# Layer norms between VectorE and ScalarE in a cross-attention and FFN kernel: passes moved, two waits placed elsewhere, a new end

## The chip, the cores and the metric

The kernel runs on one core of one Trainium2 chip. The metric is the device time of one execution in microseconds. Three runs of the kernel before give a median of 678.73 us (675.15 to 682.0).

## The reference

What is computed, for 8 batch rows of 100 query tokens and 722 context tokens, model width 512, 16 heads of 32:

```python
x = x + xattn(layernorm(x), ctx, ctx)      # q, k, v projections with bias, 16 heads
#   scores = q k^T / sqrt(32);  attn = sparsemax(scores);  out = (attn v) Wo + bo
h = layernorm(x)
x = x + sqrt((h @ cos(theta + theta_noise))**2 + (h @ sin(phi + phi_noise))**2)
# layernorm(x) = (x - mean) / sqrt(var + 1e-5), no gain, no bias
```

## The kernel before, in words

**Tiling.** A batch row is 100 tokens on 100 partitions. Its context is padded to 726 and cut into KC = 6 pieces of CK = 121. K, Q and V are made per batch; K and V with operands split in two float16 terms (three matmuls for each product, line 463), the output projection (`wo`, line 514) and the FFN (`wcos`, `wsin`, line 531) in float32. The 16 heads of a batch are handled in two parts of 8. A part `i` is batch `i // 2`, heads 0 to 7 (even `i`) or 8 to 15 (odd `i`); there are NH = 16 parts.

**Phases.** Every engine has its own instruction stream, written out by hand over the same list of phases `i` = -1 to 17, with semaphores between them. `b, odd = divmod(i, 2)`. In phase `i` TensorE multiplies the scores of part `i + 1`, VectorE finds the sparsemax thresholds of part `i`, and TensorE and ScalarE attend part `i - 1`. An odd phase also makes the first half of K and all of Q of batch `b + 1`, and the second layer norm's transposes and the FFN of batch `b - 1`. An even phase makes the second half of K and all of V of batch `b`, and the output projection of batch `b - 1`.

**TensorE** (`block.tensor`). `k_of`, `v_of`, `q_of`, `o_of` and `ffn_of` are generators that yield after each chunk of 128 contracted elements. `attend(i - 1)` yields 13 units: first `tau` (line 600: the thresholds are transposed into three more rows of the queries), then six blocks of scores, transposed (`st`, line 612, 8 matmuls), and six mixes with V (`mix`, line 583, 16 matmuls), each mix standing one block behind. Between the units stands `fill`: chunks of V in an even phase; in an odd one Q, the transposes of the normalised x1 (`x2T_of`, line 487) and the FFN. At the end of every phase `sum_flags(i)` (lines 542 and 544) sums VectorE's marks `over` over the partitions. Results go to two rings in PSUM, `ring1` (3 slots: projections) and `ring2` (2 slots: scores, blocks, tau), and ScalarE frees a slot by reading it (`one_read`, `two_read`).

**VectorE** (`block.vector`). For each head it takes the 8 largest of each of 16 pieces of the scores (`maxes`, line 952), then `thresholds(i)` does four turns over these candidates and marks, in line 988, which are above the threshold (`flag_ready`). In the next phase `read_flags` and `settle` look whether a head needs all its 722 scores after all. Three heads do in these inputs: they are refined one after the other (line 1029), two of them in phase 4 and one in phase 11, while TensorE waits in line 600 for `verified`. VectorE also does both layer norms: `stats` (bn_stats, bn_aggr, lines 928 and 930) and `normalise` (reciprocal and `(x - mean) * inv`, lines 934 and 936). For the first norm (`ln1`, tile xq, batch `b + 1`) they stand after head 4 and after the thresholds of the even phase; for the second (`ln2`, tile x1, batch `b - 1`) after heads 3 and 5 of the odd phase.

**ScalarE** (`block.scalar`) reads PSUM: K (lines 700, 704), V, Q and the scores S (`copy`, line 692), relu of the blocks to pT (line 817), attended values to aT (line 800). It makes the high float16 half of the context (`high_ctx`), the square root of the norms' variance (`ln_sd`, line 769), and square and root of the FFN (lines 782, 786).

**GpSimd** (`block.gpsimd`) makes the low halves (`low_ctx` line 340, `low_k` line 348, `low_q`), splits the thresholds (`split_tau`, lines 388 to 396), adds the bias to the residual (`residual`, line 362), makes x1 (`attended_x`, line 369), the FFN's sum of squares (line 374) and the output (`y_of`, line 379). SyncE's queue issues the transfers: kst, the context, xq, xr, and the store of `att`.

Two lines say how TensorE weaves an odd phase:

```python
fill = chain(itertools.islice(queries, 3), x2, queries, ffn)
for n, _ in enumerate(units):
    run(fill, (2, 1, 1, 1, 1, 0, 1, 0, 1, 0, 0, 0, 0)[n])
```

## Time and profile before

| | |
|---|---|
| median of 3 runs | 678.73 us (675.15 to 682.0) |
| profiled execution | 676.18 us |
| its span | 674.4 us |
| mean granted TensorE clock | 0.915 of full |
| chain that ended last, by engine | PE 49%, DVE 26%, issue 11%, ACT 7%, SPq 4%, DMA 2%, POOL 1% |
| longest kinds of TensorE's waits | line 600 42.3 us in 3; line 542 for VectorE 11.4 us in 6 |

The span runs from the first to the last instruction that the profiler shows; the time of the execution has 1.8 us more around it. The chain is followed back from the last instruction to what released it each time. PE is TensorE, PEld its weight loads, DVE VectorE, ACT ScalarE, POOL GpSimd, SPq the queue that SyncE feeds. A time in brackets in a list by time is how long the engine had stood idle, with what released it; "issue" is idle time for which the profile shows no releaser. A granted clock of 1.00 is 2.4 GHz, 0.50 is 1.2 GHz.

### The profile page before, as it was taken

To read this page: it belongs to the slowest core of one execution; us is meant where nothing else is said; L and a number is where in the kernel's file an instruction comes from. 1 tells how busy PE (TensorE), PEld (TensorE's weight loads), DVE (VectorE), ACT (ScalarE), POOL (GpSimd) and SP (SyncE) were. 2 spreads that over 40 slices of the span, in tenths; PEclk is the share of its full clock that TensorE was granted. 3 is DMA by queue.
4 is the path that set the end of the run, shared out by engine and by line. 5 is a ranking of instruction groups with operands and counts; after the bars stand their busy time and mean duration, and the time that the engine had idled before them with its cause. 6 is when DMAs were issued, how large, how long until landed. Compare 5 with 4: busy or idle time off the path is not lost.

```text
span 674.4 us, 14485 instructions
## 1 busy us (share of the span) xinstructions
PE 571.3 (85%) x4648; PEld 336.7 (50%) x4648; DVE 573.3 (85%) x2900; ACT 378.0 (56%) x657; POOL 189.0 (28%) x239
## 2 busy tenths in 40 slices
PE   2686999999913999899999999991899999988675
PEld 1343665656502655565556555651556565645431
DVE  5699999978967999999999999995999999999400
ACT  3674568767511667566756676661466666554321
POOL 2711322332220250435133422342024431310301
PEclk9968987999965999999999999996899999996768
DMA  9863022302230103130323022302203020300000
GB/s 309 273 173 91 16 63 74 96 7 62 84 84 0 31 11 98 55 98 5 85 69 105 0 61 89 103 11 61 76 9 98 20 54 27 80 7 9 13 1 12
DMA packets 33506, 44.25 MB, mean 66 GB/s; under 512 B 8386, under 2 KB 26818, under 8 KB 33415
## 3 DMA queue, kind: packets, MB, share of 16 engines
q1 hardware_dynamic: 32332, 41.16, 21.4%
q10 hardware_dynamic: 1088, 2.10, 0.9%
q8 instruction: 37, 0.61, 0.4%
q14 instruction: 49, 0.39, 0.2%
HBM read 23.77 MB, written 1.64 MB: 38 GB/s over the span
## 4 chain that ended last, share of the span: by engine, by line
PE 49%; DVE 26%; issue 11%; ACT 7%; SPq 4%; DMA 2%; POOL 1%; DVEq 0%; POOLq 0%; ACTq 0%
PE ring L463 29%; DVE cand L952 7%; PE mix_bank L583 3%; PE ring L612 3%; DVE dif L966 3%; PE ring L514 3%; PE ring L558 3%; DVE f_sum L975 3%; SPq L255 3%; DVE over L969 3%; ACT S L692 3%; PE ring L531 2%; DVE n_over L977 2%; DVE dif L970 2%; PE ring L501 1%
## 5 line engine op out<-in xcount | busy, mean ns | idle before, releaser
L952 DVE MAX8 cand<-S 100x8 f32<-100x45 f32 (+1 forms) x2048 | 223.5, 195 | 2.1 <-issue 0.4
L463 PE MATMUL ring<-wv,ctx 128*121 128x512 f16 x576 | 154.5, 390 | 0.0
L463 PE MATMUL ring<-ctx,wk 128*128 128x361 f16 x768 | 125.7, 323 | 4.7 <-DVE ctx L1118 4.7
L817 ACT ACTIVATE pT<-ring 121x800 f32<-121x800 f32 x96 | 80.5, 839 | 72.3 <-PE ring L612 71.6
L692 ACT ACTIVATE S<-ring 100x722 f32<-100x722 f32 x128 | 95.5, 773 | 32.6 <-PE ring L558 32.6
L463 PEld LDWEIGHTS ring<-ctx,wk 128*128 128x128 f16 x768 | 75.1, 99 | 50.0 <-issue 7.1
L340 POOL TENSOR_TENSOR ctx<-ctx_f,ctx 128x484 f16<-128x484 f32 x42 | 51.5, 1225 | 149.8 <-ACT ctx L692 149.4
L463 PEld LDWEIGHTS ring<-wv,ctx 128*121 128x121 f16 x576 | 71.4, 136 | 34.0 <-issue 7.7
L348 POOL TENSOR_TENSOR ks<-k_f,ks 128x361 f16<-128x361 f32 x64 | 57.9, 905 | 79.6 <-ACT k_f L704 76.7
L558 PE MATMUL ring<-kst,qst 96*100 96x361 f16 x256 | 65.1, 348 | 11.5 <-DMA kst<-ks 8.9
L612 PEld LDWEIGHTS ring<-qst,kst 99*121 99x121 f16 x768 | 59.3, 147 | 29.7 <-issue 13.8
L700 ACT ACTIVATE ks<-ring,bk_c 128x361 f16<-128x361 f32 x64 | 36.0, 563 | 65.3 <-PE ring L463 65.3
L612 PE MATMUL ring<-qst,kst 99*121 99x100 f16 x768 | 64.3, 231 | 2.9 <-ACT qst L692 2.9
L583 PE MATMUL mix_bank<-pT,v 121*32 121x100 f32 x1536 | 56.8, 269 | 1.9 <-ACT aT L800 1.2
L558 PEld LDWEIGHTS ring<-kst,qst 96*100 96x100 f16 x256 | 30.8, 133 | 55.3 <-issue 21.5
L692 ACT ACTIVATE qst<-ring 96x800 f16<-96x800 f32 (+1 forms) x32 | 25.7, 829 | 49.6 <-PE ring L600 45.9
L966 DVE TENSOR_TENSOR dif<-cand,tau 100x256 f32<-100x256 f32 (+1 forms) x64 | 51.3, 801 | 2.2
L583 PEld LDWEIGHTS mix_bank<-pT,v 121*32 121x32 f32 x1536 | 34.0, 115 | 35.4 <-issue 30.7
L975 DVE TENSOR_REDUCE f_sum<-dif 100x8 f32<-100x256 f32 (+1 forms) x64 | 49.7, 777 | 0.0
L600 PE MATMUL ring<-ident,tt 100*3 100x100 f16 x128 | 9.5, 225 | 46.0 <-issue 42.3
L374 POOL TENSOR_TENSOR sq<-sq 100x512 f32<-100x512 f32 x8 | 10.1, 1264 | 112.9 <-ACT sq L782 112.9
L969 DVE TENSOR_SCALAR over<-dif 100x256 bf16<-100x256 f32 (+1 forms) x64 | 38.4, 601 | 2.2
(124 smaller groups left out, 722.9 us busy)
## 6 DMA issues: line engine op xcount, KB each, us to landing
kst<-ks SPq DMA_DIRECT2D x384, 45.1 KB, 1.9
ctx_f<-in_ctx SPq DMA_DIRECT2D x45, 242.0 KB, 2.9
xq<-in_x SPq DMA_DIRECT2D x8, 200.0 KB
xr<-in_x SPq DMA_DIRECT2D x8, 200.0 KB
out_y<-att SPq DMA_DIRECT2D x8, 200.0 KB
S<-in_L_xattn_Wk ACTq DMA_DIRECT2D x1, 1024.0 KB, 6.9
wq<-in_L_xattn_Wq ACTq DMA_DIRECT2D x1, 1024.0 KB, 11.4
wcos<-in_L_ffn_theta SPq DMA_DIRECT2D x1, 1024.0 KB, 10.4
```

Of the source, the lines that this page charges most:

```text
L340: pool.tensor_tensor(ctx2[:, 1, :, at], ctx_f[:, n % 3, :, :], ctx2[:, 0, :, at], ALU.subtract).then_inc(ctx_lo_ready, 1)
L348: pool.tensor_tensor(ks[:, n % 2, 1, at], k_f[:, u % 2, :], ks[:, n % 2, 0, at], ALU.subtract).then_inc(k_lo_ready, 1)
L463: last = nc.tensor.matmul(psum, lhs(c, i), w(c, j), start=(c == 0 and n == 0), stop=(c == DC - 1 and n == 2))
L558: last = nc.tensor.matmul(psum[0:L, half, 0:HALF], qst[0:3 * DH, b % 2, HH * part + h, :], kst[0:3 * DH, i % 3, h, half * HALF:(half + 1) ...
L583: last = nc.tensor.matmul(mix_ps[DH * j:DH * (j + 1), :], v[0:CK, i % 3, kc, DH * (G * g + j):DH * (G * g + j + 1)], pT[0:CK, st_unit(i, g ...
L612: last = nc.tensor.matmul(psum[0:CK, c, j * L:(j + 1) * L], kst[0:99, i % 3, G * g + j, kc * CK:(kc + 1) * CK], qst[0:99, b % 2, HH * part ...
L692: return nc.scalar.activation(dst, src, ACT.Copy, **kw)
L817: nc.scalar.activation(pT[0:CK, u % 3, :, :], src, ACT.Relu).then_inc(two_read, 1)
L952: last = nc.vector.max(pieces[:, h, :, n], S[0:L, HH * (i % 2) + h, cuts[n]:cuts[n + 1]])
L966: n = counted(nc.vector.tensor_tensor(dif[:, :, 0:E], cand[:, :, 0:E], t3.broadcast_to([L, HH, E]), ALU.subtract))
L969: n_mask = counted(nc.vector.tensor_scalar(over[:, :, 0:E], dif[:, :, 0:E], 0.0, None, ALU.is_ge))
L975: counted(nc.vector.reduce_sum(f_sum[:, :], dif[:, :, 0:E], AX))
```

## The change

1. **Layer norms on ScalarE.** For ln1 of batches 1 to 7 and ln2 of batches 0 to 6 ScalarE does `centre` (a pass that sums x times -1/D into the mean with its results going to a tile nobody reads, one that subtracts the mean, one that sums the squares, and the root; each waits for the one before) and later `scale_x` or `scale_x1` (one pass, times the reciprocal). VectorE only makes the reciprocals (`invert`), after head 7 of the even phase (ln1) and after head 5 of the odd one (ln2). The first ln1 and the last ln2 stay on VectorE.
2. **Two waits.** TensorE sums the marks of an odd phase after the first four chunks of K of the next phase, no longer at the end of its own. GpSimd waits for the marks of the even phase before the last three of its six `low_ctx`.
3. **New end.** In the last attended phase the four chunks of `wo` stand between the units (each waits for its own aT), the FFN of batch 6 moves behind all units of its phase, and VectorE makes the last x1 straight from PSUM, and the last two additions, where ScalarE and GpSimd did.

The diff, cut to its core:

```diff
@@ gpsimd
-                    if 0 <= b - 1 < B:
+                    if 0 <= b - 1 < B - 1:
                         sum_squares(b - 1)
...
                         for kc in range(KC):
+                            if kc == KC // 2:
+                                pool.wait_ge(flag_ready, 2 * b + 1)
                             low_ctx(b + 1, kc)
                     if b > 0:
                         residual(b - 1)
+                    if 0 < b < B:
                         attended_x(b - 1)
-            y_of(B - 1)
@@ tensor
             def o_of(b):
...
-                pe.wait_ge(aT_ready, DC * (b + 1))
                 psum = slot1(("o", b))[0:L, :]
                 for c in range(DC):
+                    pe.wait_ge(aT_ready, DC * b + c + 1)
...
-                    fill = chain(itertools.islice(queries, 3), x2, queries, ffn)
+                    idle = iter([None] * (0 if b + 1 < B else 2))
+                    fill = chain(itertools.islice(queries, 3), x2, queries, idle, ffn)
...
                     weave(heads, fill, 1)
-                    if 0 <= i < NH:
-                        sum_flags(i)
                 else:
                     if b < B:
                         run(k_of(b, 2, 0), 4)
+                    if i > 0:
+                        sum_flags(i - 1)
+                    if b < B:
                         run(k_of(b, 2, 1), 4)
...
+                    attended_o = o_of(b - 1) if b > 0 else iter(())
                     run(fill, 4)
+                    if b == B:
+                        run(attended_o, 1)
                     for n, _ in enumerate(units):
                         run(fill, 2 if n == 0 else 1)
+                        if b == B and n in (0, 10):
+                            run(attended_o, 1)
                     weave(heads, fill, 1)
-                    if b > 0:
-                        run(o_of(b - 1), 4)
+                    run(attended_o, 4)
@@ scalar
+            def ln_link(ins):
+                ins.then_inc(ln_step, 1)
+                ln_steps[0] += 1
+                act.wait_ge(ln_step, ln_steps[0])
+
+            def centre(src, dst, mv, sd, done):
+                ln_link(nc.scalar.activation(unread[:, :], src, ACT.Copy, scale=-1.0 / D, accum_out=mv[:, 0:1]))
+                ln_link(nc.scalar.activation(dst, src, ACT.Identity, bias=mv[:, 0:1]))
+                ln_link(nc.scalar.activation(unread[:, :], dst, ACT.Square, accum_out=mv[:, 1:2]))
+                nc.scalar.activation(sd[:, 0:1], mv[:, 1:2], ACT.Sqrt, bias=eps_t[:, :], scale=1.0 / D).then_inc(done, 1)
+
+            def centre_x1(b):
+                act.wait_ge(x1_ready, b + 1)
+                centre(x1[:, :], x2n, mv2, sd2, ln2_sd)
+
+            def scale_x1(b):
+                act.wait_ge(ln2_inv, b + 1)
+                nc.scalar.activation(x2n, x2n, ACT.Identity, scale=sd2[:, 1:2]).then_inc(x2n_ready, 1)
...
-                    if 0 <= b - 1 < B:
-                        ln_sd(b - 1, mv2, sd2, ln2_stat, ln2_sd)
+                    if 0 <= b - 1 < B - 1:
+                        centre_x1(b - 1)
+                    if b == B:
+                        ln_sd(mv2, sd2, ln2_stat, ln2_sd)
                     run(units, 3)
+                    if 0 <= b - 1 < B - 1:
+                        scale_x1(b - 1)
                     if 0 <= b - 1 < B:
                         x2T_of(b - 1)
...
                     if b + 1 < B:
-                        ln_sd(b + 1, mv1, sd1, ln1_stat, ln1_sd)
+                        centre_x(b + 1)
                     run(units, 2)
...
-                    if b > 0:
+                    if b + 1 < B:
+                        scale_x(b + 1)
+                    if 0 < b < B:
                         o_of(b - 1)
@@ vector
+            def invert(b, sd, sd_done, done):
+                dve.wait_ge(sd_done, b + 1)
+                nc.vector.reciprocal(sd[:, 1:2], sd[:, 0:1]).then_inc(done, 1)
...
+            def last_x():
+                dve.wait_ge(one_full, one["o", B - 1] + 1)
...
+                nc.vector.tensor_tensor(x1[:, :], ring1[0:L, one["o", B - 1] % 3, :], xr[:, :], ALU.add).then_inc(one_read, 1)
...
                     if h == 3 and i > 0:
                         read_flags(i - 1)
-                    if h == 3 and odd and b >= 1:
-                        ln2_stats(b - 1)
                     if h == 4 and i > 0:
                         settle(i - 1)
                     if h == 5 and odd and b >= 1:
-                        ln2_apply(b - 1)
-                    if h == 4 and not odd and b + 1 < B:
-                        ln1_stats(b + 1)
+                        invert(b - 1, sd2, ln2_sd, ln2_inv)
+                    if h == HH - 1 and not odd and b + 1 < B:
+                        invert(b + 1, sd1, ln1_sd, ln1_inv)
                 thresholds(i, found)
                 if i == 0:
                     part_turns(1, wsin)
-                if not odd and b + 1 < B:
-                    ln1_apply(b + 1)
             read_flags(NH - 1)
             settle(NH - 1)
-            ln2_stats(B - 1)
-            ln2_apply(B - 1)
+            last_x()
+            last_norm()
+            last_y()
```

`scale_x` and `centre_x` are the same two functions for xq, with `ln1` semaphores.

How the instructions stand on ScalarE in an odd phase, from the last K of the phase to the second copy after the blocks. `ks` and `k_f` are K, `qst` with 3 rows the copied thresholds, `pT` the blocks, `k_f` 128x400 the transposed x2n. Before:

```order
L700 ACTIVATE ks<-ring,bk_c 128x361
L704 ACTIVATE k_f<-ring,bk_c 128x361
L769 ACTIVATE sd<-mv,eps_t 100x1
L692 ACTIVATE qst<-ring 3x800
L817 ACTIVATE pT<-ring 121x800 x2
L692 ACTIVATE k_f<-ring 128x400
```

and after the change (line numbers are those of the new file; `sq` here is x2n):

```order
L710 ACTIVATE ks<-ring,bk_c 128x361
L714 ACTIVATE k_f<-ring,bk_c 128x361
L791 ACTIVATE unread,mv<-x 100x512
L792 ACTIVATE sq<-x,mv 100x512
L793 ACTIVATE unread,mv<-sq 100x512
L794 ACTIVATE sd<-mv,eps_t 100x1
L702 ACTIVATE qst<-ring 3x800
L858 ACTIVATE pT<-ring 121x800 x2
L810 ACTIVATE sq<-sq,sd 100x512
L702 ACTIVATE k_f<-ring 128x400
```

Three passes now stand ahead of the root and of `qst`, and one ahead of the copy of the transposed x2n. The order of the rest is as before.

TensorE from the last unit of phase 15 to the end of its stream. `n_over` and `over` are the marks, `ident,tt` is tau, `qst,kst` a block, `pT,v` a mix, `wo` the output projection, `ident,sq` the transposes of x2n, `wcos` and `wsin` the FFN. Before (the blocks and mixes between are the same):

```order
L583 MATMUL mix_bank<-pT,v 32x100 x16
L531 MATMUL ring<-wcos,k_f 100x512 x2
L531 MATMUL ring<-wsin,k_f 100x512 x4
L542 MATMUL mix_bank<-n_over,ones 1x8
L544 MATMUL mix_bank<-over,minus_b 1x8x16 x7
L544 MATMUL mix_bank<-over,one_b 1x8x16
L600 MATMUL ring<-ident,tt 3x100 x8
L612 MATMUL ring<-qst,kst 121x100 x16
...
L612 MATMUL ring<-qst,kst 121x100 x8
L583 MATMUL mix_bank<-pT,v 32x100 x16
L514 MATMUL ring<-wo,aT 100x512 x4
```

and after:

```order
L587 MATMUL mix_bank<-pT,v 32x100 x16
L535 MATMUL ring<-wcos,k_f 100x512 x4
L535 MATMUL ring<-wsin,k_f 100x512 x4
L546 MATMUL mix_bank<-n_over,ones 1x8
L548 MATMUL mix_bank<-over,minus_b 1x8x16 x7
L548 MATMUL mix_bank<-over,one_b 1x8x16
L518 MATMUL ring<-wo,aT 100x512
L604 MATMUL ring<-ident,tt 3x100 x8
L518 MATMUL ring<-wo,aT 100x512
L616 MATMUL ring<-qst,kst 121x100 x16
...
L518 MATMUL ring<-wo,aT 100x512
L587 MATMUL mix_bank<-pT,v 32x100 x16
L518 MATMUL ring<-wo,aT 100x512
```

All four chunks of wcos stand behind the units now, not two, and three chunks of wo stand ahead of the last two mixes.

## Rows read from the trace of the kernel before

**Rows 1.** The page, part 1: busy us, share of the span, instructions.
```profile
PE 571.3 (85%) x4648; PEld 336.7 (50%) x4648; DVE 573.3 (85%) x2900; ACT 378.0 (56%) x657; POOL 189.0 (28%) x239
```

**Rows 2.** Busy time by stretch: one quiet odd phase, the even phase after it.
```profile
311.22:342.90 31.68, 30.09 (x276) 17.62 (x276) 30.07 (x146) 21.61 (x36) 8.31 (x12) 1.00 0.26 73
342.90:380.49 37.59, 37.22 (x306) 22.31 (x306) 36.53 (x202) 23.41 (x46) 14.76 (x18) 1.00 0.21 57
```

**Rows 3.** TensorE by time: start us, us; in brackets idle before, releaser.
```profile
213.03 0.83 PE L600 MATMUL ring<-ident,tt 100*3 100x100 f16 x8 [25.18 <-issue]
...
342.90 0.20 PE L542 MATMUL mix_bank<-n_over,ones 100*1 100x8 f32 x2 [1.57 <-DVE over L988]
...
473.84 0.82 PE L600 MATMUL ring<-ident,tt 100*3 100x100 f16 x8 [15.55 <-issue]
```

**Rows 4.** VectorE by time, the same odd phase.
```profile
321.27 0.82 DVE L936 TENSOR_SCALAR sq<-x,mv,sd 100x512 f32<-100x512 f32 x1
...
341.62 1.22 DVE L988 TENSOR_TENSOR over<-cand,tau 100x1024 bf16<-100x1024 f32 x1
```

**Rows 5.** ScalarE by time, the same odd phase.
```profile
320.68 0.29 ACT L769 ACTIVATE sd<-mv,eps_t 100x1 f32<-100x1 f32 x1
320.99 0.83 ACT L692 ACTIVATE qst<-ring 3x800 f16<-3x800 f32 x1
...
323.90 0.84 ACT L817 ACTIVATE pT<-ring 121x800 f32<-121x800 f32 x1 [0.51 <-PE ring L612]
```

**Rows 6.** TensorE by time, the same odd phase.
```profile
321.91 0.62 PE L612 MATMUL ring<-qst,kst 99*121 99x100 f16 x8
...
323.27 0.60 PE L612 MATMUL ring<-qst,kst 99*121 99x100 f16 x8
323.70 0.53 PE L487 MATMUL ring<-ident,sq 100*128 100x100 f32 x4
```

**Rows 7.** Groups by line and shape; last, a VectorE instruction by time.
```profile
L340 POOL TENSOR_TENSOR ctx<-ctx_f,ctx 128x484 f16<-128x484 f32 x42 | 51.5, 1225 | 149.8 <-ACT ctx L692 149.4
...
L966 DVE TENSOR_TENSOR dif<-cand,tau 100x512 f32<-100x512 f32 x16 | 11.1, 692 | 0.5
...
L786 ACT ACTIVATE sq<-sq 100x512 f32<-100x512 f32 x8 | 5.0, 628 | 2.8 <-POOL sq L374 2.8
...
L1006 DVE DVE_READ_ACCUMULATOR dif<-dif,delta,zero 100x1 f32 x6 | 0.5, 81 | 0.0
...
193.11 0.91 DVE L995 TENSOR_SCALAR_CACHE_REDUCE over<-dif 100x722 bf16<-100x722 f32 x1 [0.45 <-DVE dif L1006]
```

**Rows 8.** ScalarE and TensorE by time, the even phase.
```profile
359.31 0.30 ACT L769 ACTIVATE sd<-mv,eps_t 100x1 f32<-100x1 f32 x1
359.92 0.84 ACT L817 ACTIVATE pT<-ring 121x800 f32<-121x800 f32 x1 [0.31 <-PE ring L612]
...
362.84 0.55 PE L583 MATMUL mix_bank<-pT,v 121*32 121x100 f32 x16
```

**Rows 9.** TensorE by time, the last stage.
```profile
630.80 0.20 PE L542 MATMUL mix_bank<-n_over,ones 100*1 100x8 f32 x2 [3.51 <-DVE over L988]
...
633.14 0.82 PE L600 MATMUL ring<-ident,tt 100*3 100x100 f16 x8 [1.55 <-issue]
...
646.62 6.19 PE L514 MATMUL ring<-wo,aT 128*100 128x512 f32 x8 [0.46 <-ACT aT L800]
```

**Rows 10.** GpSimd by time, the end.
```profile
653.57 1.26 POOL L369 TENSOR_TENSOR x<-att,xr 100x512 f32<-100x512 f32 x1 [18.74 <-issue]
```

**Rows 11.** TensorE by time, phases 0 and 1.
```profile
65.25 0.51 PE L558 MATMUL ring<-kst,qst 96*100 96x361 f16 x2 [2.40 <-DMA kst<-ks]
...
95.28 0.89 PE L583 MATMUL mix_bank<-pT,v 121*32 121x100 f32 x16 [1.20 <-ACT aT L800]
```

**Rows 12.** Busy of PE, PEld, DVE, ACT, POOL; then granted clock, DMA.
```profile
95.00:96.00 1.00, 0.71 (x16) 0.53 (x16) 1.00 (x2) 0.96 (x2) 0.61 (x1) 0.67 0.21 54
...
109.00:110.00 1.00, 1.00 (x9) 0.61 (x7) 1.00 (x11) 0.99 (x2) 0.00 (x0) 1.00 0.00 0
```

More of the change, by code:

```diff
@@ L204, in build_kernel @@
         step, fix, check_step = sem("step"), sem("fix"), sem("check_step")
-        ln1_stat, ln1_sd, xn_ready = sem("ln1_stat"), sem("ln1_sd"), sem("xn_ready")
-        ln2_stat, ln2_sd, x2n_ready = sem("ln2_stat"), sem("ln2_sd"), sem("x2n_ready")
+        ln1_stat, ln1_sd, ln1_inv, xn_ready = (sem(n) for n in ("ln1_stat", "ln1_sd", "ln1_inv", "xn_ready"))
+        ln2_stat, ln2_sd, ln2_inv, x2n_ready = (sem(n) for n in ("ln2_stat", "ln2_sd", "ln2_inv", "x2n_ready"))
+        ln_step = sem("ln_step")
         res_ready, x1_ready, sqsum_ready, root_ready, y_ready = (
@@ L765, in o_of, with ln_sd, centre_x, scale_x @@
                 copy(att[:, :], src).then_inc(one_read, 1)
-            def ln_sd(b, mv, sd, stat, done):
-                act.wait_ge(stat, b + 1)
+            def ln_sd(mv, sd, stat, done):
+                act.wait_ge(stat, 1)
                 nc.scalar.activation(sd[:, 0:1], mv[:, 1:2], ACT.Sqrt, bias=eps_t[:, :]).then_inc(done, 1)
+            ln_steps = [0]
+            def ln_link(ins):
[7 more added lines that the diff above has]
+                nc.scalar.activation(sd[:, 0:1], mv[:, 1:2], ACT.Sqrt, bias=eps_t[:, :], scale=1.0 / D).then_inc(done, 1)
+            def centre_x(b):
+                act.wait_ge(in_xq, 16 * (b + 1))
+                centre(xq[:, :], xq[:, :], mv1, sd1, ln1_sd)
+            def scale_x(b):
+                act.wait_ge(ln1_inv, b)
+                nc.scalar.activation(xq[:, :], xq[:, :], ACT.Identity, scale=sd1[:, 1:2]).then_inc(xn_ready, 1)
+            def centre_x1(b):
[4 more added lines that the diff above has]
+                nc.scalar.activation(x2n, x2n, ACT.Identity, scale=sd2[:, 1:2]).then_inc(x2n_ready, 1)
             def x2T_of(b):
@@ L830, in _ @@
             act.wait_ge(dve_const, 3)
-            ln_sd(0, mv1, sd1, ln1_stat, ln1_sd)
+            ln_sd(mv1, sd1, ln1_stat, ln1_sd)
             for kc in range(KC):
@@ L1083, in settle, with last_y, last_norm, first_norm @@
                     dve.sem_inc(verified, 1)
-            def ln2_stats(b):
-                dve.wait_ge(x1_ready, b + 1)
-                stats(b, x1, st2, mv2, ln2_stat)
-            def ln2_apply(b):
-                if b > 0:
-                    dve.wait_ge(root_ready, b)
-                normalise(b, x1, mv2, sd2, x2n, ln2_sd, x2n_ready)
+            def last_x():
+                dve.wait_ge(one_full, one["o", B - 1] + 1)
+                dve.wait_ge(one_read, one["o", B - 1])
+                dve.wait_ge(res_ready, B)
+                dve.wait_ge(y_ready, B - 1)
+                nc.vector.tensor_tensor(x1[:, :], ring1[0:L, one["o", B - 1] % 3, :], xr[:, :], ALU.add).then_inc(one_read, 1)
+            def last_y():
+                dve.wait_ge(one_read, seen1(("ffn", B - 1, 1)))
+                nc.vector.tensor_tensor(sq[:, 1, :], sq[:, 0, :], sq[:, 1, :], ALU.add).then_inc(sqsum_ready, 1)
+                dve.wait_ge(root_ready, B)
+                dve.wait_ge(stored, 16 * (B - 1))
+                nc.vector.tensor_tensor(att[:, :], x1[:, :], sq[:, 0, :], ALU.add).then_inc(y_ready, 1)
+            def last_norm():
+                dve.wait_ge(one_read, seen1(("o", B - 1)))
+                stats(x1, st2, mv2, ln2_stat)
+                dve.wait_ge(root_ready, B - 1)
+                normalise(B - 1, x1, mv2, sd2, x2n, ln2_sd, x2n_ready)
+            def first_norm():
+                dve.wait_ge(in_xq, 16)
+                stats(xq, st1, mv1, ln1_stat)
+                normalise(0, xq, mv1, sd1, xq[:, :], ln1_sd, xn_ready)
             def link(ins, n):
@@ L1136, in _ @@
             after(n)
-            ln1_stats(0)
-            ln1_apply(0)
+            first_norm()
             split_weight(0, wk2, wk_f, in_wk)
```

8 lines of the change are left out of this document (2 added, 6 removed).

## The prediction

> **What bounds the kernel now.** First the page: VectorE and TensorE are both busy 85% of the span, ScalarE 56%, GpSimd 28% [rows 1]. That names no bound, so I went on to the chain of waits and from it to the stages. A batch row takes two phases. In the middle of the run, where nothing is refined, an odd phase lasts 31.68 us and an even one 37.59 us [rows 2], together 69.27. TensorE is busy for 30.09 and 37.22 us of them: it is full in the even phase, and in the odd one it has a single wait, 1.57 us at its end, for VectorE's marks [rows 3]. Beside that wait, which comes back in every quiet odd phase, its large ones are the refinements, 25.18 and 15.55 us [rows 3]. VectorE is almost gapless: ScalarE's square root ends at 320.97 [rows 5], then come reciprocal and scaling, two heads of MAX8 and the thresholds, and the marks are ready at 342.84 [rows 4]; TensorE goes on 0.06 us later. So TensorE's own stream sets the period (69.27 - 1.57 = 67.7 us), and VectorE holds it up by 1.57. That is the first fact: relief of VectorE can give back 1.57 us per quiet batch and not more.
>
> The second fact is ScalarE's place in TensorE's odd phase. It makes the 0.29 us root at 320.68, copies the thresholds (qst) at 320.99, and turns the second block of scores into pT at 323.90 [rows 5]. TensorE starts its first block (L612) at 321.91, and qst was done at 321.82. The transposes of x2n (L487) follow the second block after 0.43 us [rows 6]. There is 0.1 us of slack: what ScalarE does ahead of 320.99 moves TensorE.
>
> **Odd phases.** centre_x1 puts three passes over 100x512 ahead of the root. The nearest row for such a pass from SBUF is L786, 0.628 us [rows 7]; the root is 0.29; each step waits for the one before, 0.06 as above; each of the two sums may need a read of 0.08, as VectorE's does [rows 7]. 3 x 0.63 + 0.29 + 3 x 0.06 + 2 x 0.08 = 2.52 us, where 0.31 stood. Less 0.1 of slack the first block comes **2.1 us** later. From below the bound is 1.9 (sums for nothing), from above 2.9: after its sum VectorE's next instruction waited 0.45 [rows 7], and two of these in place of 2 x 0.08 add 0.7. The Trainium skill speaks against the move (ScalarE: Activation LUTs, section Rules for kernel authors): it wants additions and multiplications on VectorE, and budgets 0.3 us plus 0.83 ns an element for an ACTIVATE, for 512 elements an estimate of 0.72. By that this term would be 2.4. The row says 0.63, and the row is used.
>
> scale_x1 stands behind the second pT; the reciprocal on VectorE is done long before. pT starts 0.63 after its block (323.90 for 323.27) and lets the next instruction start 0.74 later; a pass of 0.63 and 0.04 behind it, and the transposes of x2n can start 2.04 us after the second block, not 0.43: **1.6 us** more. It can't be less than the pass itself, 0.6; TensorE's queue is in order, and the first mix stands behind the transposes.
>
> Removed is the wait. The marks of an odd phase are now summed behind the first twelve matmuls of the next (about 1.9 us). The marks came 21.87 us after the root; without VectorE's scaling of 0.82 [rows 4] it is 21.0. The root is now at 11.9 us of the phase, the marks at 32.9; TensorE ends the phase at 30.1 + 3.7 = 33.8 and asks at 35.7. So 1.57 us go. Net 2.1 + 1.6 - 1.6 = **+2.1 us** in each of the four quiet odd phases: +8.5. What VectorE saves (the 0.82 here, and about as much for each of the other scaling and the two statistics, 4 us per batch less its old wait) is gained by nobody: it stands at its two reciprocals until ScalarE's roots are there.
>
> The phase before the first refinement: its end comes from VectorE, whose chain starts with the root, 2.1 later and 0.8 shorter: +1.3. In the phase of the 15.55 us wait the centring is hidden in it, and only the transposes come about 1.3 later. Together **+2.6**.
>
> **Even phases.** centre_x stands where a root stood, at 359.31; the third pT then starts not at 359.92 but at about 361.8 and ends at 362.7, and TensorE's mix wants it at 362.84 [rows 8]. It fits, barely. I take 0.2 in each of seven, **+1.5** in all; bounds 0 and 5 (dear sums: 0.7 each). scale_x at the end finds ScalarE idle. GpSimd's new wait pushes three subtractions of ctx behind VectorE's marks. They take 1.2 us each [rows 7], and TensorE needs the last some 6 us after the marks. Nothing; behind them are the two residual additions and the first subtractions of k, whose transfers TensorE needs only at the end of its next phase. If ScalarE runs 2 us later than I have it, TensorE waits here too.
>
> **The end.** In phase 15 TensorE was early and waited 3.51 us for the marks [rows 9]. VectorE loses statistics and scaling there, -2.2. But the ffn matmuls, a part of which stood between the mixes, now stand behind them, and the centring delays the blocks; at half clock TensorE would be 1.0 later than the marks were. Between -2.2 and +1.0 I take **-0.6**. After the marks:
> - attend(15), from the copy of tau at 633.14 to wo at 646.62, ran at half clock, 13.5 us [rows 9]. A block takes 0.43 us at full clock [rows 6], half as long as here, while ScalarE's passes stay: about 9.5 us with three of the four wo chunks inside, -4.0. At half clock the chunks would add 1.5.
> - wo took 6.19 us [rows 9]; only a quarter stays behind the last mix: 1.55 at half clock or 0.8 at full, so -4.6 or -5.4.
> - x1 comes from PSUM on VectorE (0.69, as L966 at this size [rows 7]), not by a copy at 652.8 and a GpSimd addition that ends at 654.83 [rows 10]: -1.3. The two last additions: 0.69 for 1.26 each, -1.1.
> Full clock: -11.8. Half: -5.5. As the ffn matmuls now reach up to the marks, TensorE doesn't idle 3.5 us ahead of this stage, so I take **-11.8**, and leave the last ffn as it is.
>
> **The clock in the odd phases** has no row. TensorE gets gaps of 2.1 and 1.6 us with little between them. In phase 1 the clock fell from 2.4 to 1.2 GHz behind 95.28, after a wait of only 1.20 us which followed two microseconds of blocks and mixes alone [rows 11], and was back at 109 [rows 12]. A gap of 2.40 us between dense matmuls, at 65.25, cost nothing [rows 11]. The new gaps have f32 matmuls on both sides, which is nearer to the second. I take two falls in five phases, 1.7 us each: **+3.4**. Bounds: 0, and 34 (five times half of phase 1's 13.7).
>
> **Sum**: 8.5 + 2.6 + 1.5 - 0.6 - 11.8 + 3.4 = +3.6 us. The profiled execution took 676.2 us (the span of 674.4 and 1.8 around it), 2.5 under the median of the runs. On that median, 678.7 + 3.6 = 682.
>
> **The rivals.**
> A. The centring is hidden, and VectorE's relief counts: five times 1.57, 2.2 in phase 15, 11.8 in the end, -22, so 657 us. For it: ScalarE is idle 44% of the span. Against it: not in the places where the passes stand [rows 5, 6]. 13%.
> B. The other side: the clock falls in every odd phase and stays low for some 8 us, 4 us lost each, 20 instead of 3.4: 699. Without falls the sum is +0.2, so from two falls of this length on the change is slower by over 1%. For it: phase 1. Against it: the gap at 65.25. 23%.
> C. The sums are dear: +0.7 in five odd phases and, the even phases' margin being used up, +0.6 in seven: +8, 690. 11%.
> D. The forecast, by itself 673 to 691: 53%. A half-clock end is in it (+6).
>
> About 1% is what a measurement of this kernel tells from no change, so 671.9 to 685.5 is the same. Faster: A and 0.09 of D, 0.22. Slower: B, most of C (0.09) and 0.05 of D, 0.37. The same: 0.41. The range, 666 to 697, leaves out A and the upper half of B.
>
> **What would show it.** In the new profile: TensorE idle about 2.1 us before the first block of each odd phase, released by ScalarE's qst, and 1.6 before the transposes of x2n, released by ScalarE's scaling; no wait at the flags; VectorE idle for microseconds at its reciprocals; odd phases of 33.8 us, even ones of 37.8; the granted clock between them (B); one wo chunk behind the last mix, 0.43 a matmul or 0.85. If TensorE waits for nobody in an odd phase, A holds and the forecast is wrong at its first term.

## The result, and the profile after

The changed kernel takes 700.4 us (median of 4 runs, 697.9 to 701.9); the kernel before took 677.7 (4 runs) beside it. The ratio is 1.033, 95% interval 1.026 to 1.039: slower. The forecast of 682 and its range end of 697 were too low. The profiled execution took 700.8 us with a span of 699.0, 24.6 more than the span before.

The page of the changed kernel: part 1, the row of the granted clock over 40 slices, and the chain by engine.

```profile
PE 589.4 (84%) x4648; PEld 344.8 (49%) x4648; DVE 551.5 (79%) x2861; ACT 416.6 (60%) x740; POOL 180.9 (26%) x236
...
PEclk9879989998966987999899999997799978997757
...
PE 65%; issue 14%; ACT 10%; SPq 6%; DMA 2%; DVE 1%; POOL 1%; POOLq 0%; ACTq 0%; DVEq 0%
```

VectorE works 21.8 us less than in [rows 1], and ScalarE 38.6 more. The chain of what ended last holds 1% of VectorE. So VectorE was relieved, and the time grew: what ends last is now TensorE behind ScalarE. TensorE's own busy time rose by 18.1 us for the same 4648 matmuls, and its mean granted clock fell from 0.915 to 0.895: some of them ran at the lower clock.

Busy time by stretch (PE, PEld, DVE, ACT, POOL; then granted clock, DMA share, GB/s), to be read beside [rows 2]: an odd phase with a fall of the clock, an even phase, an odd phase without a fall.

```profile
321.98:360.90 38.92, 35.37 (x289) 20.37 (x288) 36.45 (x217) 24.81 (x42) 10.94 (x15) 0.91 0.21 60
360.90:396.66 35.76, 35.39 (x296) 21.14 (x296) 26.12 (x129) 25.92 (x51) 11.44 (x15) 1.00 0.21 59
396.66:432.54 35.88, 32.33 (x289) 18.86 (x289) 33.38 (x188) 24.59 (x42) 10.40 (x14) 1.00 0.24 65
```

The flags of an odd phase are now summed twelve matmuls into the next, so the border between the two has moved by 1.9 us; only the pair can be compared. Without a fall it is 35.88 us and 35.75 for the even phase behind it, 71.63 together; before it was 69.27. TensorE is idle for 3.55 us of this odd phase.

ScalarE by time, the odd phase from 321.98 on; it answers to [rows 5].

```profile
331.44 0.63 ACT L791 ACTIVATE unread<-x 100x512 uint8<-100x512 f32 x1
331.96 0.20 ACT L791 ACTIVATION_READ_ACCUMULATOR unread<-x 100x1 f32 x1
332.19 0.72 ACT L792 ACTIVATE sq<-x,mv 100x512 f32<-100x512 f32 x1
332.95 0.63 ACT L793 ACTIVATE unread<-sq 100x512 uint8<-100x512 f32 x1
333.48 0.19 ACT L793 ACTIVATION_READ_ACCUMULATOR unread<-sq 100x1 f32 x1
333.70 0.29 ACT L794 ACTIVATE sd<-mv,eps_t 100x1 f32<-100x1 f32 x1
334.02 0.83 ACT L702 ACTIVATE qst<-ring 3x800 f16<-3x800 f32 x1
...
336.93 0.84 ACT L858 ACTIVATE pT<-ring 121x800 f32<-121x800 f32 x1 [0.50 <-PE ring L616]
337.66 0.71 ACT L810 ACTIVATE sq<-sq,sd 100x512 f32<-100x512 f32 x1
```

TensorE by time, the same phase; it answers to [rows 6].

```profile
334.90 0.65 PE L616 MATMUL ring<-qst,kst 99*121 99x100 f16 x8 [1.95 <-ACT qst L702]
...
336.29 0.60 PE L616 MATMUL ring<-qst,kst 99*121 99x100 f16 x8
338.43 0.56 PE L491 MATMUL ring<-ident,sq 100*128 100x100 f32 x4 [1.54 <-ACT sq L810]
...
342.93 1.07 PE L616 MATMUL ring<-qst,kst 99*121 99x100 f16 x8
343.79 1.99 PE L535 MATMUL ring<-wcos,k_f 128*100 128x512 f32 x2
```

From 331.44 to 334.02 ScalarE is at the centring, 2.58 us, and the copy of qst stands behind it. TensorE shows both holes (stretches in which it stands idle): 1.95 us for qst, 1.54 for the scaling. Counted from the start of the phase, the first block comes 12.92 us in and no longer 10.69, 2.23 later, and the transposes of x2n follow the second block after 2.14 us and no longer 0.43, 1.71 later. Some two microseconds behind the second hole the clock goes from 2.4 to 1.2 GHz; the eight block matmuls at 342.93 take 1.07 us, those at 336.29 took 0.60. Three windows of the same phase show how long; the middle one has a mean clock of 0.53.

```profile
321.98:340.40 18.42, 14.89 (x115) 8.82 (x115) 16.60 (x134) 11.02 (x21) 9.26 (x14) 0.99 0.17 43
340.40:347.30 6.90, 6.90 (x61) 4.06 (x60) 6.66 (x15) 3.48 (x6) 1.68 (x1) 0.53 0.31 76
347.30:360.90 13.60, 13.58 (x116) 7.49 (x115) 13.18 (x70) 10.31 (x15) 0.00 (x0) 1.00 0.22 76
```

Of the five odd phases whose centring isn't covered by a refinement four have such a fall, two of them twice as long (phases 3 and 7: 38.24 and 38.92 us; 5 and 13: 41.37 each, at a mean clock of 0.83; phase 9: none, 35.88). Only in phase 7 does it come behind the second hole. In phases 3, 5 and 13 the clock is already down behind the first: the transposes take 0.93 us there, for 0.56. TensorE in phase 5:

```profile
257.78 0.75 PE L616 MATMUL ring<-qst,kst 99*121 99x100 f16 x8 [1.96 <-ACT qst L702]
...
262.67 0.93 PE L491 MATMUL ring<-ident,sq 100*128 100x100 f32 x4 [1.54 <-ACT sq L810]
```

The end. TensorE by time, and the end in three windows; they answer to [rows 9].

```profile
659.37 0.20 PE L546 MATMUL mix_bank<-n_over,ones 100*1 100x8 f32 x2
...
663.07 0.52 PE L604 MATMUL ring<-ident,tt 100*3 100x100 f16 x8 [1.98 <-POOLq L400]
...
664.52 1.88 PE L616 MATMUL ring<-qst,kst 99*121 99x100 f16 x16
...
677.69 2.03 PE L518 MATMUL ring<-wo,aT 128*100 128x512 f32 x2 [0.46 <-ACT aT L841]
```

```profile
659.37:664.70 5.33, 3.35 (x25) 1.55 (x25) 1.45 (x3) 2.06 (x3) 3.86 (x8) 0.97 0.01 2
664.70:684.21 19.51, 15.30 (x154) 9.89 (x152) 2.27 (x5) 6.50 (x10) 1.05 (x1) 0.50 0.04 11
684.21:699.00 14.79, 9.11 (x16) 3.24 (x16) 1.38 (x2) 1.82 (x3) 0.00 (x0) 0.85 0.05 14
```

The wait of 3.51 for the marks is gone, and one wo chunk is behind the last mix, as meant. But the last half's attention and wo ran at 1.2 GHz again. From the marks to the end it is 39.63 us for 43.60.

In place of the old wait stands a new one, 1.98 us at tau, for GpSimd's split of the thresholds. The FFN's matmuls now reach up to the marks, so GpSimd gets the FFN's squares only then, and their sum stands ahead of the split in its stream:

```profile
660.15 1.26 POOL L376 TENSOR_TENSOR sq<-sq 100x512 f32<-100x512 f32 x1 [24.91 <-ACT sq L823]
661.51 0.23 POOL L390 TENSOR_SCALAR t_rest<-tau 100x8 f32<-100x8 f32 x1
```

From the marks' sum to tau it is 3.70 us for 2.34 in [rows 9].

### The profile page after: what moved, and what is told of

Its sections match the earlier page's. It is cut to its first block, busy times and chain, and to the rows that moved or that the text cites. A ratio compares the mean times of both kernels' runs of the same rounds, so it can differ in the third digit from the quotient of the medians.

```text
span 699.0 us, 14518 instructions
## 1 busy us (share of the span) xinstructions
PE 589.4 (84%) x4648; PEld 344.8 (49%) x4648; DVE 551.5 (79%) x2861; ACT 416.6 (60%) x740; POOL 180.9 (26%) x236
## 4 chain that ended last, share of the span: by engine, by line
PE 65%; issue 14%; ACT 10%; SPq 6%; DMA 2%; DVE 1%; POOL 1%; POOLq 0%; ACTq 0%; DVEq 0%
PE ring L467 30%; PE ring L535 8%; PE ring L616 7%; PE mix_bank L587 6%; PE ring L562 5%; SPq L257 4%; PE ring L518 4%; PE ring L505 3%; ACT S L702 2%; SPq L261 2%; ACT qst L702 1%; PE ring L491 1%; ACT pT L858 1%; PE mix_bank L548 1%; DMA S<-in_L_xattn_Wk 1%
## 5 line engine op out<-in xcount | busy, mean ns | idle before, releaser
L467 PE MATMUL ring<-ctx,wk 128*128 128x361 f16 x768 | 127.5, 324 | 4.5 <-DVE ctx L1180 4.5
L342 POOL TENSOR_TENSOR ctx<-ctx_f,ctx 128x484 f16<-128x484 f32 x42 | 47.9, 1140 | 169.8 <-DVE over L1032 85.0
L616 PEld LDWEIGHTS ring<-qst,kst 99*121 99x121 f16 x768 | 64.4, 158 | 44.2 <-ACT qst L702 19.7
L616 PE MATMUL ring<-qst,kst 99*121 99x100 f16 x768 | 69.5, 242 | 11.8 <-ACT qst L702 11.8
L587 PE MATMUL mix_bank<-pT,v 121*32 121x100 f32 x1536 | 59.7, 280 | 2.5 <-ACT pT L858 1.2
L587 PEld LDWEIGHTS mix_bank<-pT,v 121*32 121x32 f32 x1536 | 36.1, 120 | 38.3 <-issue 29.3
L988 DVE RECIPROCAL sd<-sd 100x1 f32<-100x1 f32 x14 | 2.3, 161 | 52.4 <-ACT sd L794 52.4
L702 ACT ACTIVATE v<-ring 121x256 f32<-121x256 f32 x96 | 31.4, 384 | 13.8 <-PE ring L467 13.8
```

Source lines behind the costliest of these rows:

```text
L342: pool.tensor_tensor(ctx2[:, 1, :, at], ctx_f[:, n % 3, :, :], ctx2[:, 0, :, at], ALU.subtract).then_inc(ctx_lo_ready, 1)
L467: last = nc.tensor.matmul(psum, lhs(c, i), w(c, j), start=(c == 0 and n == 0), stop=(c == DC - 1 and n == 2))
L587: last = nc.tensor.matmul(mix_ps[DH * j:DH * (j + 1), :], v[0:CK, i % 3, kc, DH * (G * g + j):DH * (G * g + j + 1)], pT[0:CK, st_unit(i, g ...
L616: last = nc.tensor.matmul(psum[0:CK, c, j * L:(j + 1) * L], kst[0:99, i % 3, G * g + j, kc * CK:(kc + 1) * CK], qst[0:99, b % 2, HH * part ...
L702: return nc.scalar.activation(dst, src, ACT.Copy, **kw)
```

## The experiments

Theory 1, from the traces: x1's centring and scaling on ScalarE open two holes in TensorE's odd phase, and the granted clock falls behind them. Its main rival: the flags' new place or GpSimd's wait (which has x1 ready 5.0 us into the odd phase and not 2.4) costs the time.

**Norms back (e1_norms_back).** The changed kernel with the layer norms of batches 1 to 15 on VectorE; new end and both waits stay.

```diff
-centre_x1(b - 1)                      # ScalarE, odd phase
+ln_sd(b - 1, mv2, sd2, ln2_stat, ln2_sd)
...
-scale_x1(b - 1)
...
-centre_x(b + 1)                       # ScalarE, even phase
+ln_sd(b + 1, mv1, sd1, ln1_stat, ln1_sd)
...
-scale_x(b + 1)
...
-invert(b - 1, sd2, ln2_sd, ln2_inv)   # VectorE
+ln2_stats(b - 1)                      # the same for x
+ln2_apply(b - 1)
```

> The changed kernel with the layer norms of batches 1 to 15 back on VectorE (bn_stats, bn_aggr, reciprocal, one tensor_scalar); the new end and both waits stay. Theory 1 (ScalarE's passes ahead of qst and ahead of the transposes of x2n open two holes of 1.95 and 1.54 us in TensorE's odd phase, and the granted clock falls there in four phases, some 16 us): all of this goes, the odd phases keep the clock at 1.0, the sum is at most that of the kernel before less 4 for the end: 666 to 676 us. Rival (GpSimd's wait at the ctx subtractions, which has x1 ready 5.0 us into the odd phase and not 2.4, or the flags' new place costs the time): it stays at 690 to 700 us.

Measured: 665.5 us (4 runs), ratio to before 0.980 [0.977, 0.984]; theory 1's range began at 666. The change holds a gain of 14 us and a loss of 35. One pair of phases and the end:

```profile
377.41:409.29 31.88, 31.86 (x288) 18.78 (x287) 30.79 (x162) 21.68 (x36) 9.23 (x13) 1.00 0.25 73
409.29:445.05 35.76, 35.39 (x296) 21.15 (x296) 34.76 (x189) 23.34 (x45) 13.10 (x17) 1.00 0.22 60
...
626.37:663.50 37.13, 26.21 (x190) 14.15 (x190) 4.25 (x10) 9.78 (x15) 4.71 (x8) 0.76 0.04 12
```

TensorE is busy for 31.86 of 31.88 us, and the clock stays up. The pair is 67.64, against 67.7 for TensorE's own stream in the prediction. So the norms cost a clean pair 4.0 us (71.63 less 67.64), and not 2.4: the rest had been paid by the wait that goes.

**Norms only (e2_norms_only).** The kernel before, with the layer norms of the changed one and nothing else.

```diff
-ln_sd(b - 1, mv2, sd2, ln2_stat, ln2_sd)   # ScalarE; the same for x
+centre_x1(b - 1)
...
+scale_x1(b - 1)
...
-ln2_stats(b - 1)                           # VectorE; the same for x
...
-ln2_apply(b - 1)
+invert(b - 1, sd2, ln2_sd, ln2_inv)
```

> The kernel before with the layer norms on ScalarE and nothing else: old end, flags at the end of the phase, no wait on GpSimd. Theory 1: the two holes and the falls of the clock are there, and the end's gain is not: 698 to 705 us. Rival (the new end and the waits cost the time): within 5 us of the kernel before, about 680.

Measured: 712.3 us (4 runs), ratio 1.048 [1.043, 1.054]. The rival falls. It is dearer than theory 1 has it, by 7 us above its range. The clock isn't the reason: with 34.0 to 35.7 us the odd phases lose less by it than in the changed kernel. But the even phases grew from 37.59 [rows 2] to 39.78, and TensorE waits 2.12 us at their end for VectorE's marks, where it didn't before. And one half of theory 1 does not hold here: the same two holes are there (2.07 and 1.54 us in phases 5, 7 and 9, some 1.7 and 1.54 in 3 and 13), and behind them the clock falls in none of the five. The falls that three of these phases have come at their start, behind the wait of 2.12 us, and cost 1.6 us each.

**No wait on GpSimd (e5_no_gpsimd_wait).** The changed kernel but for

```diff
 for kc in range(KC):
-    if kc == KC // 2:
-        pool.wait_ge(flag_ready, 2 * b + 1)
     low_ctx(b + 1, kc)
```

> The changed kernel without GpSimd's wait for the flags in the middle of the ctx subtractions. x1 is ready 2.6 us earlier in the odd phase. Theory 1 (centring starts only when ScalarE has made the eviction of the last K block, so that x1's time does not matter): within 2 us of the changed kernel, the falls of the clock as they are, 698 to 702. Rival (the wait is the cause): 680 to 690. A rival on the other side: GpSimd's subtractions meet VectorE's work at the end of the even phase again, and the time rises by up to 5 us.

Measured: 709.6 us (4 runs, 701.4 to 715.5), ratio 1.041 [1.034, 1.048]: 9 us above the changed kernel, by runs that lie far apart; the two intervals overlap, so the size is open. The profile is of the 715.5. It has even phases of 37.95 us for 35.75, with TensorE waiting 2.12 at their end for the marks. So the rival on the other side holds, and the wait that I had priced at nothing looks like a gain; e13_spread_no_wait below is the clear case. x1 comes earlier, and no odd phase is shorter for it: a clean one is 35.88, as in the changed kernel.

**Holes filled (e3_gaps_filled).** The changed kernel with matmuls whose result isn't read, in TensorE's odd phase.

```diff
 for n, _ in enumerate(units):
+    if n == 2 and 0 < b < B:
+        keep_busy(15)
     run(fill, (2, 1, 1, 1, 1, 0, 1, 0, 1, 0, 0, 0, 0)[n])
+    if n == 0 and 0 < b < B:
+        keep_busy(19)        # 128 x 240, f16
```

> The changed kernel with matmuls whose result nobody reads in both holes of the odd phases from batch 1 on: 19 of 128 x 240 columns ahead of the first block, 15 ahead of the transposes of x2n (about 2.3 and 1.9 us of TensorE at full clock). They cost little more than the holes that they fill, 0.7 us a batch at most. Theory 1 with the granted clock as the larger part: the clock stays at 1.0 in the odd phases, the time falls by some 16 us to about 684 to 688. Rival (the holes themselves, or work later in the phase, cost the time and the clock is a sign of it): 700 to 710 us, no less than the changed kernel.

Measured: 681.8 us (10 runs; nine of them 679.4 to 683.6, one 1619, which I can't explain), ratio 1.003 [0.999, 1.006], a little under the expected 684. The mean clock of those nine is 0.93 to 0.94, that of the changed kernel's four 0.89 to 0.90. Every odd phase from 3 on whose centring no refinement covers is clean:

```profile
317.63:353.50 35.87, 35.80 (x322) 22.04 (x321) 33.38 (x188) 24.57 (x42) 10.41 (x14) 1.00 0.23 65
...
646.12:679.60 33.48, 22.11 (x190) 10.84 (x190) 4.25 (x10) 9.56 (x15) 4.71 (x8) 0.85 0.05 13
```

Its odd phase takes 35.87 us, as long as the clean one of the changed kernel, with 34 matmuls more: the fill costs nothing. By phases the changed kernel is above it by 2.36, 5.49, 3.05, 0 and 5.50 in the odd ones (16.4), by 1.9 in phase 15 and by 6.2 in the end. So the clock's share is shown: some 16 us in the odd phases, and more at the end. These sum to more than the 19.4 us between the two spans, because 5.0 net go the other way: the part ahead of phase 1, in which the programs are the same, took 2.4 more with the fill, and phases 4 and 11, with the refinements, are 1.5 shorter each in the changed kernel. In phase 4 that takes back most of what the fall in phase 3 had cost. The 4.0 us of the holes stay.

**One hole filled (e11_first_hole, e12_second_hole).** The same with keep_busy(19) alone, and with keep_busy(15) alone.

> The changed kernel, only the first hole of the odd phases filled (19 matmuls ahead of the first block). Theory (each hole alone is too short to bring the clock down, both together with the light matmuls between them do): the clock stays at 1.0, as with both filled: 680 to 688 us. Rival (the second hole, the last before the clock falls, is enough): 695 to 702 us.

> The changed kernel, only the second hole filled (15 matmuls ahead of the transposes of x2n). Theory as for the first hole alone: 680 to 688 us. Rival (the first hole, the longer one, sets the fall off): 695 to 702 us.

Measured: 689.9 us, 1.018 [1.014, 1.022], and 691.9, 1.020 [1.016, 1.024]. Neither theory's number: both lie between. In the profiles a single hole still brings the clock down, in one of five odd phases behind the second hole (1.54 us; phase 5) and in three behind the first (1.80 to 1.98), but each fall costs only 1.5 us (37.3 to 37.4 for 35.9), not 2.4 to 5.5. The three are phases 3, 5 and 13, those in which the changed kernel's clock was down behind the first hole too. So the first hole starts most of the falls, and with the second open as well they last longer: the mean clock of such a phase is 0.83 or 0.91, and 0.95 here. What else they are above 681.8 lies for the most part in phase 15 and the end. A sharp condition can't be read from this.

**Which norm (e6_x_only).** x1's norm back on VectorE, x's norm still on ScalarE.

```diff
-centre_x1(b - 1)                       # ScalarE
...
+nc.scalar.activation(sd2[:, 0:1], mv2[:, 1:2], ACT.Sqrt, bias=eps_t[:, :]).then_inc(ln2_sd, 1)
...
-scale_x1(b - 1)
...
+stats(x1, st2, mv2, ln2_stat)          # VectorE
...
-invert(b - 1, sd2, ln2_sd, ln2_inv)
+normalise(b - 1, x1, mv2, sd2, x2n, ln2_sd, x2n_ready)
```

> The changed kernel with only x1's norm back on VectorE; x's norm stays on ScalarE, in the even phases, where its passes lie beside the V blocks. Theory 1 (all 35 us between the run with both norms back, 665.5, and the changed kernel, 700.4, come from x1's passes in the odd phase): 663 to 668 us, even phases 35.75, odd phases 31.9 as with both norms back. Rival (VectorE's wait of 4 to 5 us for the root of x's variance, ahead of its last heads of the even phase, makes its thresholds late): TensorE waits for the marks again, 672 to 685 us.

Measured: 668.0 us, 0.983 [0.977, 0.988]. Of the 35 us, 32 go with x1's norm. x's norm costs 2.5 at most: even phases 35.75, odd ones 32.8 to 33.3 for 31.9. There TensorE waits 0.7 to 0.9 us at tau for GpSimd's split of the thresholds, which stands behind what GpSimd's new wait put off, and up to 0.4 for VectorE's marks. The rival, with its 672 to 685 us, falls.

**Passes spread (e7_spread).** The changed kernel with x1's passes in ScalarE's idle times between the K evictions, and the scaling directly behind the copy of qst.

```diff
     k_of(b + 1, 0, 0)
     k_of(b + 1, 1, 0)
+    next(parts, None)        # the sum of x1
     k_of(b + 1, 0, 1)
     xT_of(b + 1)
+    next(parts, None)        # x1 less its mean
     k_of(b + 1, 1, 1)
+for _ in parts:              # squares, root
+    pass
...
-centre_x1(b - 1)
...
-run(units, 3)
+run(units, 1)
 scale_x1(b - 1)
+run(units, 2)
```

> The changed kernel with x1's passes on ScalarE spread over its idle times between K evictions: the sum of x1 after the second K block, the centring after x's transposes, the squares and the root after the last K block; the scaling directly behind the copy of qst and not behind the second copy of pT. Theory 1: qst's copy comes 1.2 to 1.4 us earlier, the first hole shrinks from 1.95 to 0.6 or so, the second goes with it or shrinks to under 1; the clean odd phase goes from 35.9 to 32.5 to 34 us, and the clock falls in fewer phases or none: 670 to 685 us. Rival (the sum of ScalarE's work counts, wherever it stands, since the K evictions are late instead): odd phases of 35.9, 695 to 705 us.

Measured: 665.7 us (4 runs), 0.981 [0.975, 0.987], below its expected range. ScalarE by time, and the odd phase:

```profile
384.85 0.63 ACT L812 ACTIVATE unread<-x 100x512 uint8<-100x512 f32 x1
385.37 0.20 ACT L812 ACTIVATION_READ_ACCUMULATOR unread<-x 100x1 f32 x1
385.80 0.56 ACT L710 ACTIVATE ks<-ring,bk_c 128x361 f16<-128x361 f32 x1 [0.23 <-PE ring L467]
...
389.65 0.29 ACT L821 ACTIVATE sd<-mv,eps_t 100x1 f32<-100x1 f32 x1
389.97 0.83 ACT L702 ACTIVATE qst<-ring 3x800 f16<-3x800 f32 x1
390.82 0.72 ACT L825 ACTIVATE sq<-sq,sd 100x512 f32<-100x512 f32 x1
```

```profile
379.44:412.07 32.63, 32.12 (x288) 18.79 (x287) 31.64 (x171) 24.35 (x42) 10.55 (x14) 1.00 0.25 71
```

The sum lies in 0.8 us that ScalarE had stood idle before the third K eviction. One hole of 0.46 us is left, there is no second, and no odd phase from 3 to 13 has a fall but the one with the refinement. The instructions are the same and so is ScalarE's work; 35 us went by their place. That confirms theory 1 from the other side: without the holes neither their 4.0 us a pair nor the falls are there.

**The wait on GpSimd again (e8_norms_back_no_wait, e13_spread_no_wait).** The wait taken away from the kernel with the norms back, and from the one with the passes spread (the diff of e5_no_gpsimd_wait on each).

> Both norms back on VectorE, new end, flags of the even phase one place later, but no wait on GpSimd. Theory 2 (GpSimd's ctx subtractions beside VectorE's thresholds make both slower, and GpSimd's wait ends that; 9 us in the changed kernel): TensorE waits for the marks in one phase of each pair again, 1.5 to 2.2 us each, and the time is 674 to 681 us. Rival (GpSimd's wait is worth something only with the norms on ScalarE): 664 to 668 us.

> The kernel with x1's passes spread, without GpSimd's wait. With the passes in a row that wait was worth 9 us, with the norms on VectorE nothing. Theory 3 (the wait helps only where VectorE stands idle for ScalarE's root and has no slack left for its thresholds beside GpSimd; spreading makes the root 1.2 us earlier only): TensorE waits up to 2 us a pair for the marks again: 672 to 682 us. Rival (the 9 us came from x1's late sum and the holes): 664 to 668 us.

Measured: 666.1 us (4 runs), 0.980 [0.974, 0.986], and 681.5 (10 runs), 1.004 [1.002, 1.007]. With VectorE's own norms the wait is worth nothing (theory 2 falls there, and the flags' new place alone ends TensorE's 1.57); with x's norm on ScalarE it is worth 16 us. VectorE and GpSimd by time in an even phase of e13_spread_no_wait:

```profile
372.82 0.16 DVE L1005 RECIPROCAL sd<-sd 100x1 f32<-100x1 f32 x1 [3.78 <-ACT sd L792]
...
390.20 0.93 DVE L1042 SCALAR_TENSOR_TENSOR step_t<-f_sum,step_t 100x8 f32<-100x8 f32 x1
391.16 0.17 DVE L1047 SCALAR_TENSOR_TENSOR tau<-step_t,tau 100x8 f32<-100x8 f32 x1
391.36 2.18 DVE L1049 TENSOR_TENSOR over<-cand,tau 100x1024 bf16<-100x1024 f32 x1
```

```profile
390.04 1.07 POOL L342 TENSOR_TENSOR ctx<-ctx_f,ctx 128x484 f16<-128x484 f32 x1 [2.43 <-ACT ctx L700]
...
391.19 1.27 POOL L364 TENSOR_TENSOR xr<-xr,bo_b 100x512 f32<-100x512 f32 x1
```

VectorE stands 3.78 us at its reciprocal until ScalarE's root of x's variance is there, and starts its thresholds late. Then GpSimd's operations hold up one VectorE instruction each: 0.93 us where its like takes 0.17 (from 390.20 to 391.13, when the subtraction of 390.04 is over), the marks 2.18 for 1.22. Five instructions are so, 4.2 us together; with the wait one of the five is still there (1.00 for 0.17). GpSimd is held up too: the addition of x1 behind the marks takes 2.13 us, for 1.27 with the wait. TensorE then waits 2.12 us at the marks, and an even phase takes 37.94 for 35.75. With the wait the last three subtractions come behind the marks. The Trainium skill has this (SBUF — State Buffer, section SBUF: two separate sides): VectorE and GpSimd share a port pair, and of a GpSimd operation and a VectorE one with two inputs in SBUF the one that starts first holds it for the whole instruction. The trace agrees for the instruction at 390.20, which has two such inputs: it ends within 0.02 us of the subtraction.

The 2.12 us cost twice. In four of the five odd phases behind them the clock is down for the first microseconds, 1.6 us each (34.2 to 34.3 for 32.6), although dense matmuls stand ahead of the wait and, after 1 us of the marks' sums, behind it. The start of phase 7 (the clock is the third number from the end):

```profile
321.41:325.20 3.79, 3.79 (x21) 2.18 (x22) 3.74 (x35) 0.00 (x0) 1.07 (x1) 0.55 0.02 4
```

**The end (e9_end_filled, e10_spread_filled).** Unread matmuls in the last phases: on the kernel with norms back, 36 while TensorE waits for tau and 14 in the end; on the spread one, 19 and 15 of them in phase 15, between the light matmuls.

```diff
+if b >= B - 1:                             # e9, ahead of the units
+    keep_busy(36 if b == B - 1 else 14, ("x2T", b - 1))
...
+if n == 0 and b == B - 1:                  # e10, as in e3_gaps_filled
+    keep_busy(19)
+if n == 2 and b == B - 1:
+    keep_busy(15)
```

> Both norms back on VectorE, and matmuls that nobody reads (128 x 240) where TensorE waits in the last phases: 36 while it waits for tau of the half before the last, 14 while it waits for x1's norm in the end. Theory (a filled hole keeps the granted clock at 1.0 through the light matmuls after it): the last phase before the end goes from 28.6 to about 26 us and the end from 37.1 to 34 to 36: 659 to 663 us. Rival (the clock falls in the light matmuls themselves): 665 us as without them.

> The kernel with x1's passes spread (665.7 us), and unread matmuls in the phase before the end alone: 19 behind the transposes of tau and 15 ahead of the transposes of x2n. In the changed kernel with both holes filled everywhere, that phase took 25.9 us and the end 33.5; with the passes spread they took 26.6 and 37.0. Theory: dense work between the light matmuls keeps the clock at 1.0 there: 659 to 663 us. Rival (the clock of the end comes and goes by itself: with x's norm alone on ScalarE the end took 33.6 with no filler): 664 to 667 us.

Measured: 662.6 us (4 runs), 0.974 [0.967, 0.980], and 661.4 us (5 runs), 0.975 [0.972, 0.978]. Both lie in the range of their theory, the first by luck: in e9's profile phase 15 and the end are what they were without the fill (28.58 and 37.19 for 28.59 and 37.13), so the fill doesn't explain its 3 us, and its rival holds. The spans of the two profiles differ by 1.9 us, and ahead of phase 1, where the programs are the same, e9's gets there 2.2 us earlier. e10's:

```profile
600.65:627.10 26.45, 21.07 (x217) 13.87 (x217) 25.47 (x129) 11.80 (x20) 3.12 (x7) 0.87 0.04 9
627.10:659.10 32.00, 20.67 (x190) 10.36 (x190) 4.26 (x10) 9.56 (x15) 4.72 (x8) 0.93 0.05 14
```

The end takes 32.0 us at a clock of 0.93, 11.6 less than before and 5.0 less than with the passes spread alone. Its five runs (661.0 to 662.8) all lie below the four without the fill (665.3 to 668.0), so the gain of 4 us repeats. That fill between the light matmuls holds the clock is not shown by it: the fill stands in phase 15, the gain is in the end, and the end's clock also came out at 0.85 and 0.86 with no fill (e6_x_only, 33.56 us, and e13_spread_no_wait, 33.6) and at 0.62 with the second half of it (e12_second_hole, 41.2). Both versions beat both kernels.

## Why the prediction was wrong, step by step

- **What bounds the kernel, and 1.57 us to gain**: right. With the norms back the pair is 67.64 for the 67.7 forecast.
- **First block 2.1 later, transposes 1.6 later**: right in the main, 2.23 and 1.71; as idle time of TensorE, 1.95 and 1.54. The centring took 2.58 for 2.52. Its parts were not as forecast: a sum has a read of its accumulator of 0.20 behind it (I had 0.08) that starts 0.11 before the pass ends, the pass with a bias takes 0.72 (0.63), and between dependent steps lie 0.03 and not 0.06. The errors cancel, which is luck.
- **Net +2.3 per quiet pair** (2.1 in the odd phase, 0.2 in the even): +2.36 where the clock stayed up, and all of it in the odd phase. The even phases take 35.75 us with the centring of x and without.
- **The refinements' batches +2.6**: +3.4 and +2.0. The fall of the clock in phase 3 is 2.4 of it, but phase 4 is 1.5 shorter than in e3_gaps_filled, so that some 0.8 of the fall is left.
- **Phase 15 -0.6**: +0.2 (27.77 for 27.60). The wait of 3.51 for the marks went, but the phase ran at a mean clock of 0.69 and no longer 0.81.
- **GpSimd's wait: nothing**. This failed in its reasons. I asked what the wait delays and not what it keeps apart. I also held VectorE's idle time at its reciprocals to be free; in the even phase it isn't, since it makes the thresholds late, and only this wait covers that.
- **The end -11.8**: mis-sized, -4.0. "I take full clock" failed: at half clock I had -5.5. By stretches, attention took 1.1 more (forecast 1.5 more at half clock), from wo's last stretch (before, all of wo) to the transposes of x2n 5.5 less (5.9, with x1), and the rest 1.0 less (1.1). What the sum lacked is the 1.4 ahead of tau, for GpSimd. At nearly full clock the -11.8 was a right price: e10_spread_filled has -11.6.
- **The clock in the odd phases +3.4**: this is the failed term, 16.4 measured: four falls in five phases of 2.4 to 5.5 us each, where I took two of 1.7. I had two rows for the same question, [rows 11], and chose the gap of 2.40 us between dense matmuls, which had cost nothing, as the nearer.
- That row was itself luck. The same wait, in phase 0 and for the same transfer, stands in twelve of the fourteen profiles with 2.38 to 2.58 us, and in five of them the clock fell at its end. In e1_norms_back, to be read beside [rows 11] (a row of TensorE, then a window):

```profile
65.42 0.84 PE L562 MATMUL ring<-kst,qst 96*100 96x361 f16 x2 [2.40 <-DMA kst<-ks]
65.27:68.68 3.41, 3.26 (x9) 2.02 (x10) 3.34 (x4) 1.27 (x2) 0.16 (x1) 0.50 0.26 73
```

- Phase 1's fall, the other row, was no fixed price either: with nearly the same work in that phase its mean clock is 0.81 before and 0.95 in e1_norms_back. What decides whether the clock falls behind such a gap, no run here shows; the same two holes brought it down in four of five phases in the changed kernel and in none in e2_norms_only.
- The two terms are 13.0 and 7.8 us off, together 20.8 of the 21.0 by which +24.6 differs from +3.6; of the 7.8, 1.4 are GpSimd's and not the clock's. The others cancel to 0.2.
- **Rival B** (699 us, 23%) had the mechanism, the count nearly (four of five) and the price (4 us a fall; 4.1 measured). A and C don't hold: nothing of the centring was hidden, and the sums cost what was forecast.

## What to carry to other kernels

Where an instruction stands in its engine's stream counted for 35 us here, and which engine it ran on for nothing: the same three passes cost two holes in a row, and none in the idle times between evictions. A hole in TensorE's stream is to be priced twice, by its length and by the granted clock behind it. One row of one execution in which the clock stayed up, or fell, is no price for the second part: look whether the same gap does the same in other profiles. If rows disagree, the clock is the forecast's widest term and not a mean of them. When a wait is added, ask also which two engines it keeps from running side by side. And when work is moved to fill an engine's wait, follow what its result sets off on the next engine: the FFN's matmuls filled TensorE's wait for the marks, and put GpSimd's sum ahead of tau.
